# Third of four attentions in passes of 512 tokens, with keys in partitions, maxima by a product and the reciprocal through Ln and Exp

## Chip, core and metric

The kernel runs as one program on one core of a Trainium2 chip. The metric is the device time of one execution in microseconds (us), lower is better. Engines are named as in the profile: PE is TensorE's matmul, PEld its weight load, DVE is VectorE, ACT ScalarE, POOL GpSimd, SP SyncE.

## What is computed

The input x is 4 sequences of 512 tokens with 128 numbers each. Four layers follow, each an attention over a context of 77 tokens per sequence and then a mixture of 8 or 9 experts with the top 2 chosen. The change concerns the attention of layer 2, the third of four:

```python
q1, q2 = heads(x @ q1_w.T), heads(x @ q2_w.T)          # 16 heads of 8
attn1 = softmax(q1 @ k1.T * 8 ** -0.5)                 # over 77 keys
attn2 = softmax(q2 @ k2.T * 8 ** -0.5)
x = (attn1 - (lambda_1 - lambda_2 + 0.1) * attn2) @ v1
x = x * rsqrt(mean(x * x) + 1e-6) * norm_w             # over 128
return x @ proj_w.T + proj_b
```

Here the x that enters is a layer norm, and the result is added to the residual X. The mixture behind it sends each of the 2048 tokens to two experts.

## The kernel before

The 2048 tokens are 16 tiles of 128 (NT), or 4 batches of 512 (NG). Every stage is a set of functions, one for each engine, and the stages are written one after another, so each engine runs its queue in the order in which the code was written, with semaphores between the engines.

`attention_stage("L2x")` runs 32 units, one for each tile and each of the two softmaxes (`sets` is 2). In a unit, `scores` makes 128 tokens by 16 times 77 scores in four PSUM banks, in 12 products: the array is used as four row tiles of 32 (4 heads each), and each product is split into halves (`x_up`, `x_low`) for accuracy. DVE takes the maximum (`maxima`, L971) and subtracts it from PSUM into SBUF (L975), ACT takes the exponential (L1082). PE transposes the result in 11 blocks (L863), ACT copies these out of PSUM (L1105), and PE multiplies them with the values (`weighted`, L874; the array is four column tiles of 32). ACT copies the sums (L1109), PE turns them back to tokens in partitions (L884, L885), DVE divides (L996 to L1014). After the second unit of a tile the difference is squared and summed (L1019), POOL takes the power (`rms`, L1204), ACT scales, PE turns and projects (L899, L900), and DVE adds to X (L1029).

The scores of a unit wait for the DVE's last read of the unit before (`scores_used`). `lead` is the end of the projection of the queries (L693, L711, L719), written between the first units.

`sparse_route("L2f")` is written into the same loop: for groups of tiles that are done it takes statistics, normalises, makes the router's logits, chooses two experts (`choose`, `choose_second`), ranks the tokens (`ranks`, `place`, L1750) and lets POOL scatter the rows to DRAM, sorted by expert (`pool_scatter`, L1799). `parts` are the pieces of the ranking: 8, 4, 2 and 2 tiles, each with two scatters a tile. What belongs to the last tiles stands behind the loop (`late_vector`, `late_pool`), and ends with the table of tiles `tile_at` (L1873). The next stage, the mixture of layer 2, begins on the queue of SP: it reads `tile_at`, loads two packs of weights (L1984), waits for all 32 scatters and loads the sorted rows (L1990).

## Time and profile before

| | |
|---|---|
| median of 3 runs | 1149.68 us (1148.88 to 1149.77) |
| span of the profiled execution | 1167.4 us, the only time that there is of this execution |
| busy: PE, PEld | 956.1 us (82%), 805.2 us (69%) |
| busy: DVE, ACT, POOL | 619.4 us (53%), 559.0 us (48%), 399.0 us (34%) |
| granted TensorE clock, mean | 0.912 of full speed |
| head of the third attention | 500.26 to 512.6 us |
| its loop, up to the last addition to X | 512.6 to 697.55 us |
| from there to the first load of sorted rows | 697.55 to 721.1 us |

The profiled execution is 17.7 us longer than the median. Its clock is a share of the full 2.4 GHz, and in any short stretch it is either that or half of it. A busy PE includes the latency of each product, so it isn't the array at its peak. A group that is not last at the wait that matters costs nothing.

### The profile page before, as it was taken

To read this page: it belongs to the slowest core of one execution; us is meant where nothing else is said; L and a number is where in the kernel's file an instruction comes from. 1 tells how busy PE (TensorE), PEld (TensorE's weight loads), DVE (VectorE), ACT (ScalarE), POOL (GpSimd) and SP (SyncE) were. 2 spreads that over 40 slices of the span, in tenths; PEclk is the share of its full clock that TensorE was granted. 3 is DMA by queue.
4 is the path that set the end of the run, shared out by engine and by line. 5 is a ranking of instruction groups with operands and counts; after the bars stand their busy time and mean duration, and the time that the engine had idled before them with its cause. 6 is when DMAs were issued, how large, how long until landed. Compare 5 with 4: busy or idle time off the path is not lost. (4 is left out here: it accounts for less than half of the span.)

```text
span 1167.4 us, 20624 instructions
## 1 busy us (share of the span) xinstructions
PE 956.1 (82%) x7766; PEld 805.2 (69%) x7766; DVE 619.4 (53%) x1699; ACT 559.0 (48%) x1069; POOL 399.0 (34%) x394
## 2 busy tenths in 40 slices
PE   4888999999988999979888783999367875299992
PEld 3566899999976999846666562989145554288882
DVE  7876412111266343578787653444498763444443
ACT  2666644343446334357665531656245542155552
POOL 4545110000043001500110434547365555545552
PEclk9999999999998999989998875989689985599996
DMA  9999900000000000000000004655200001445543
GB/s 349 183 179 185 199 26 2 1 1 1 1 2 1 1 1 1 1 1 2 1 2 1 28 18 136 201 175 165 73 1 1 1 10 32 137 154 168 170 153 109
DMA packets 70578, 83.83 MB, mean 72 GB/s; under 512 B 5298, under 2 KB 57529, under 8 KB 70353
## 3 DMA queue, kind: packets, MB, share of 16 engines
q1 hardware_dynamic: 64336, 71.98, 26.4%
q0 software_dynamic: 4992, 8.45, 2.1%
q10 hardware_dynamic: 1152, 2.10, 0.5%
q8 instruction: 63, 1.03, 0.4%
q14 instruction: 35, 0.28, 0.1%
HBM read 52.15 MB, written 32.18 MB: 72 GB/s over the span
## 5 line engine op out<-in xcount | busy, mean ns | idle before, releaser
L2374 ACT ACTIVATE hT<-PS,par 128x512 f32<-128x512 f32 x200 | 136.4, 688 | 174.3 <-PE PS L2278 172.8
L2414 DVE SCALAR_TENSOR_TENSOR X<-PS,wts,X 128x128 f32<-128x128 f32 x272 | 76.5, 345 | 218.3 <-PE PS L2297 218.3
L1105 ACT ACTIVATE hT<-PS 116x512 f32<-116x512 f32 (+1 forms) x192 | 102.5, 561 | 108.0 <-PE PS L863 99.4
L863 PE MATMUL PS<-par,score 128*116 128x128 f32 x704 | 114.8, 303 | 23.3 <-DVE oc L1007 12.5
L2297 PEld LDWEIGHTS PS<-regA,hT 128*128 128x128 f32 x1024 | 119.1, 192 | 3.1 <-issue 0.5
L2297 PE MATMUL PS<-regA,hT 128*128 128x128 f32 x1024 | 119.5, 275 | 0.0
L863 PEld LDWEIGHTS PS<-par,score 128*116 128x116 f32 x704 | 85.2, 149 | 41.0 <-issue 31.9
L1179 POOL TENSOR_TENSOR score<-score,mx 128x1232 f32<-128x1232 f32 x32 | 72.0, 2251 | 90.3 <-DVE mx L987 90.3
L2045 PE MATMUL PS<-q_up,halves 128*112 128x256 f32 (+1 forms) x276 | 85.6, 310 | 8.8 <-DVE hT L2154 8.8
L2276 PE MATMUL PS<-x_up,w_halves 128*128 128x512 f32 x200 | 86.4, 432 | 0.2 <-ACT hT L2374 0.2
L1082 ACT ACTIVATE score<-score 128x1232 f32<-128x1232 f32 x64 | 78.3, 1223 | 10.1 <-POOL score L1179 10.1
L2277 PE MATMUL PS<-x_low,w_halves 128*128 128x512 f32 x200 | 80.0, 400 | 0.0
L2278 PE MATMUL PS<-x_up,w_halves 128*128 128x512 f32 x200 | 79.8, 399 | 0.0
L2046 PE MATMUL PS<-q_up,halves 128*112 128x256 f32 (+1 forms) x276 | 79.5, 288 | 0.0
L2047 PE MATMUL PS<-q_up,halves 128*112 128x256 f32 (+1 forms) x276 | 79.4, 288 | 0.0
L874 PE MATMUL PS<-hT,vblk 116*32 116x128 f32 x1408 | 76.8, 293 | 0.1
L2297 PEld LDWEIGHTS PS<-regB,hT 128*128 128x128 f32 x576 | 69.7, 191 | 3.1
L2297 PE MATMUL PS<-regB,hT 128*128 128x128 f32 x576 | 70.1, 275 | 0.0
L594 POOL TENSOR_TENSOR rstd<-vare,mhalf 128x4 f32<-128x4 f32 (+1 forms) x24 | 27.6, 1151 | 114.7 <-DVEq L539 114.7
L874 PEld LDWEIGHTS PS<-hT,vblk 116*32 116x32 f32 x1408 | 53.4, 115 | 18.6 <-issue 8.6
L2213 POOL DMA_INDIRECT sorted_y<-regA x46 | 47.4, 1030 | 53.1 <-DVE regA L2180 42.7
L2213 POOL DMA_INDIRECT sorted_y<-regB x46 | 45.2, 983 | 54.4 <-ACT regB L2119 46.1
(315 smaller groups left out, 2016.2 us busy)
## 6 DMA issues: line engine op xcount, KB each, us to landing
regA<-L3f_w SPq DMA_DIRECT2D x23, 704.0 KB
regB<-L2f_w SPq DMA_DIRECT2D x23, 578.0 KB
L2f_sorted_x<-empty_row SPq DMA_DIRECT2D x8, 1161.0 KB, 21.0
L3f_sorted_x<-empty_row SPq DMA_DIRECT2D x8, 1161.0 KB, 20.2
regA<-L0f_w SPq DMA_DIRECT2D x4, 768.0 KB, 16.9
regA<-L2f_sorted_x SPq DMA_DIRECT2D x23, 129.0 KB, 3.8
regB<-L3f_sorted_x SPq DMA_DIRECT2D x23, 129.0 KB, 4.1
par<-params SPq DMA_DIRECT2D x1, 2450.0 KB, 13.8
```

The lines of the kernel that those rows point to most:

```text
L863: last = nc.tensor.transpose(PS[0:BW, bank_of(("exps", 3 * u + i)), (j % 4) * P:(j % 4) * P + P], exps_of(u)[:, first:first + BW], ident)
L874: last = nc.tensor.matmul(PS[slot, 6, c:c + P], vblk[0:BW, b, j, :], hT[0:BW, u % 2, j // 4, (j % 4) * P:(j % 4) * P + P], start=half == 0 ...
L1105: nc.scalar.activation(hT[0:BW, u % 2, i, 0:width], PS[0:BW, bank, 0:width], ACT.Copy).then_inc(pT_ready.sem, 1)
L2045: nc.tensor.matmul(dst, w_up, up, start=True, stop=False)
L2046: nc.tensor.matmul(dst, w_up, low, start=False, stop=False)
L2047: last = nc.tensor.matmul(dst, w_low_half, up, start=False, stop=True)
L2213: nc.gpsimd.indirect_dma_start(sorted_y, bass.IndirectOffsetOnAxis(ap=at, axis=0), y_slots[:, i % 4, j, :], None, bounds_check=2 * B * S - ...
L2276: nc.tensor.matmul(dst, w_up, upper[:, cols], start=True, stop=False)
L2277: nc.tensor.matmul(dst, w_up, x_low[:, cols], start=False, stop=False)
L2278: last = nc.tensor.matmul(dst, w_low, upper[:, cols], start=False, stop=True)
L2297: last = nc.tensor.matmul(PS[:, 4 + n % 2, j * P:j * P + P], hT[0:rows, n % 2, k, j * P:j * P + P], w2[0:rows, e, k, :], start=k == 0, sto ...
L2374: nc.scalar.activation(hT[:, n % 2, k, :], PS[:, i % 4, :], c["act"], bias=pc(f"{tag}_b1")[:, col:col + 1]).then_inc(h_ready.sem, 1)
```

## The change

The loop of 32 units becomes 8 passes (4 batches by 2 softmaxes), each in 3 steps n, with 3 steps more at the end. In pass i, step k:

- `products` makes scores with up to 103 of the 308 rows (4 heads by 77 keys) in partitions and 512 tokens in columns: 12 products in four row tiles, one PSUM bank each, and 4 more that subtract the maximum, which is a row of `shiftT` times a table of -1 (`minus_head`).
- `exps` takes the exponential from PSUM in two instructions of 1024 columns. There are no transposes of the exponentials.
- `values` and `sums` multiply them, a step later, with the values and with a table of ones for each head, in four column tiles of 512 columns.
- The maximum itself needs scores with tokens in partitions. `maxima` makes them again, 6 products for 8 heads of one tile, 8 times a pass, into banks 4 and 5, which DVE reduces; the maxima of a pass are turned by 4 transposes (`turn`) and copied by ACT (`shift`). They are made one pass ahead.
- `reciprocal` is Ln and Exp(-x) on ACT; DVE's `divide` multiplies numerator and denominator by it, and `correct` does one correction step.
- the square sum is a product with ones, `norm_w` is folded into the projection once, and the bias is added to X by POOL ahead of the passes. Once per batch, `finish` multiplies and adds to X.
- The router's groups are four of 4 tiles, `parts` are 8, 4 and 4, and POOL scatters the 16 rows of part 0 in one piece.
- The tables `minus_head` and `head_cols` add 404 columns to the second load of parameters, and the lambdas take 30 less.

The values of layer 2 are laid out as `vwide`, in the memory of `vblk`. Nothing is changed in the other three attentions, except that layer 3 clears the padding of `vblk` again.

```diff
...
+WIDE = [103, 103, HR * K - 206]
+WIDE_AT = [0, 103, 206]
...
+        def wide_stage(tag, q_ready, kv, nm, lead, sums_read, route):
...
+            passes = B * sets
+            steps = 3 * passes
...
+            def extras(n):
+                i, k = divmod(n, 3)
+                b = finished(i)
+                parts = [[], [], []]
+                if k == 0:
+                    parts[0] += pairs(i + 1, (2,))
+                    parts[1] += pairs(i + 1, (3,))
+                if k == 1:
+                    parts[0] += pairs(i + 1, (4, 5))
+                    parts[1] += pairs(i + 1, (6,))
+                    parts[2] += pairs(i + 1, (7,))
+                    if b is not None:
+                        parts[2].append(("ss", b))
+                if k == 2:
+                    if i + 1 < passes:
+                        parts[0].append(("turn", i + 1))
+                    if b is not None:
+                        parts[0].append(("y", b))
+                    parts[1] += pairs(i + 2, (0,))
+                    parts[2] += pairs(i + 2, (1,))
+                for kind in ("rows", "logits", "ranks"):
+                    if route["due"](kind, n) is not None:
+                        parts[2].append((kind, route["due"](kind, n)))
+                return parts
...
+            head = [("max", p) for p in range(8)] + [("turn", 0)] + [("max", 8), ("max", 9)]
...
+            banks = {"max": (4, 5), "turn": (4,), "ss": (5,), "y": (5,), "rows": (4,), "logits": (5,), "ranks": (4,)}
...
+            def tensor(pe):
+                def maxima(u):
+                    i, p = divmod(u, 8)
+                    (b, s), (j, h) = divmod(i, sets), divmod(p, 2)
+                    t = TG * b + j
...
+                    up, low = q[s]
+                    for m, (half, u_k) in enumerate(((up, 0), (up, 1), (low, 0))):
+                        for r in (2 * h, 2 * h + 1):
+                            dims = slice(32 * r, 32 * r + 32)
+                            last = nc.tensor.matmul(PS[:, 4 + r % 2, 0:HR * K], half[dims, t * P:t * P + P], kb[dims, s, u_k, b, :, :],
+                                                    start=m == 0, stop=m == 2)
+                    last.then_inc(max_psum.sem, 1)
+                def turn(i):
+                    pe.wait_ge(rows_ready.sem, rows_ready.at(TG * (i + 1)))
+                    for j in range(TG):
+                        last = nc.tensor.transpose(PS[:, 4, j * P:j * P + P], max_rows[:, j, :, :].rearrange("p g c -> p (g c)"), ident)
+                    last.then_inc(turn_psum.sem, 1)
+                def products(n):
+                    i, k = divmod(n, 3)
+                    b, s = divmod(i, sets)
+                    up, low = q[s]
+                    w, at, cols = WIDE[k], WIDE_AT[k], slice(512 * b, 512 * b + 512)
+                    if n:
+                        pe.wait_ge(exp_ready.sem, exp_ready.at(n))
+                    for m, (half, u_k) in enumerate(((up, 0), (up, 1), (low, 0))):
+                        for r in range(RG):
+                            dims = slice(32 * r, 32 * r + 32)
+                            nc.tensor.matmul(PS[0:w, r, :], kb[dims, s, u_k, b, :, :].rearrange("p h k -> p (h k)")[:, at:at + w], half[dims, cols],
+                                             start=m == 0, stop=False)
+                    if k == 0:
+                        pe.wait_ge(shift_ready.sem, shift_ready.at(i + 1))
+                    for r in range(RG):
+                        dims = slice(32 * r, 32 * r + 32)
+                        last = nc.tensor.matmul(PS[0:w, r, :], minus_head[dims, at:at + w], shiftT[dims, :], start=False, stop=True)
+                    last.then_inc(prod_ready.sem, 1)
+                def values(n):
+                    i, k = divmod(n, 3)
+                    if k == 0 and i:
+                        pe.wait_ge(sums_used.sem, sums_used.at(i))
+                    pe.wait_ge(exp_ready.sem, exp_ready.at(n + 1))
+                    w = WIDE[k]
+                    for r in range(RG):
+                        nc.tensor.matmul(PS[32 * r:32 * r + 32, 6, :], vwide[0:w, k, i // sets, r, :], hT[0:w, n % 2, r, :],
+                                         start=k == 0, stop=k == 2)
+                def sums(n):
+                    k = n % 3
+                    w = WIDE[k]
+                    for r in range(RG):
+                        last = nc.tensor.matmul(PS[32 * r:32 * r + 32, 7, :], pc("head_cols", w)[:, 32 * k:32 * k + 32], hT[0:w, n % 2, r, :],
+                                                start=k == 0, stop=k == 2)
+                    last.then_inc(sums_psum.sem, 1)
...
+                for use in head:
+                    if use == ("turn", 0):
+                        pe.wait_ge(q_ready.sem, q_ready.at(sets * NG))
...
+                    do(use)
+                    if use == ("max", 1):
+                        lead["transpose_group"](pe, 3)
+                        lead["project"](pe, 2)
+                    if use == ("max", 3):
+                        lead["project"](pe, 3)
+                for n in range(steps + 3):
+                    first, middle, end = extras(n)
+                    if n < steps:
+                        products(n)
+                    for use in first:
+                        do(use)
+                    if 0 < n <= steps:
+                        values(n - 1)
+                    for use in middle:
+                        do(use)
+                    if 0 < n <= steps:
+                        sums(n - 1)
+                    for use in end:
+                        do(use)
...
+            def vector(v, st):
+                def maxima(u):
+                    i, p = divmod(u, 8)
+                    if i >= passes:
+                        return
+                    j, h = divmod(p, 2)
+                    m = mx[:, (u // 2) % 3, :]
+                    v.wait_ge(max_psum.sem, max_psum.at(u + 1))
+                    ps = PS[:, 4:6, 0:HR * K].rearrange("p r (h k) -> p r h k", h=HR)
+                    nc.vector.tensor_reduce(m[:, 8 * h:8 * h + 8].rearrange("p (r h) -> p r h", r=2), ps, AX.X, ALU.max).then_inc(max_read.sem, 1)
+                    if h == 0:
+                        return
+                    v.wait_ge(max_read.sem, max_read.at(u + 1))
+                    if i:
+                        v.wait_ge(turn_psum.sem, turn_psum.at(i))
...
+                    up = max_rows[:, j, :, 0:HR]
+                    nc.vector.tensor_copy(up.bitcast(F32R), m).then_inc(v_step, st.one())
+                    v.wait_ge(v_step, st.n)
+                    nc.vector.tensor_tensor(max_rows[:, j, :, HR:2 * HR], m, up, ALU.subtract).then_inc(rows_ready.sem, 1)
+                def divide(i):
+                    s = i % sets
+                    v.wait_ge(rec_ready.sem, rec_ready.at(i + 1))
...
+                    nc.vector.tensor_tensor(w_check, PS[:, 7, :], w_rec, ALU.mult).then_inc(v_step, st.one())
+                    if s == 0:
+                        ins = nc.vector.tensor_tensor(quotient, PS[:, 6, :], w_rec, ALU.mult)
+                    else:
+                        ins = nc.vector.scalar_tensor_tensor(quotient, PS[:, 6, :], lam[:, 0:1], w_rec, ALU.mult, ALU.mult)
+                    ins.then_inc(sums_used.sem, 1)
+                    v.wait_ge(v_step, st.n)
+                def correct(i):
+                    b, s = divmod(i, sets)
...
+                    nc.vector.scalar_tensor_tensor(quotient, w_check, 2.0, quotient, ALU.subtract, ALU.mult).then_inc(v_step, st.one())
+                    if s == 0:
+                        return
+                    v.wait_ge(v_step, st.n)
...
+                    nc.vector.tensor_tensor(w_att, w_second, w_first, ALU.subtract).then_inc(att_ready.sem, 1)
+                    v.wait_ge(att_ready.sem, att_ready.at(b + 1))
+                    nc.vector.tensor_tensor(w_sq, w_att, w_att, ALU.mult).then_inc(sq_ready.sem, 1)
...
+                def finish(b):
...
+                    v.wait_ge(y_psum.sem, y_psum.at(b + 1))
+                    for j in range(TG):
+                        t = TG * b + j
+                        nc.vector.scalar_tensor_tensor(X[:, t, :], PS[:, 5, j * P:j * P + P], osr[:, j:j + 1], X[:, t, :], ALU.mult, ALU.add)\
+                            .then_inc(x_done.sem, 1)
...
+            def scalar(a, st):
+                def exps(n, h):
...
+                    a.wait_ge(prod_ready.sem, prod_ready.at(n + 1))
+                    if n >= 2:
+                        a.wait_ge(sums_psum.sem, sums_psum.at(n - 1))
+                    ins = nc.scalar.activation(hT[0:w, n % 2, 2 * h:2 * h + 2, :], PS[0:w, 2 * h:2 * h + 2, :], ACT.Exp, scale=scale)
+                    ins.then_inc(*((exp_ready.sem, 1) if h else (a_step, st.one())))
+                def shift(i):
+                    a.wait_ge(turn_psum.sem, turn_psum.at(i + 1))
+                    nc.scalar.activation(shiftT[:, :], PS[:, 4, :], ACT.Copy).then_inc(shift_ready.sem, 1)
+                def reciprocal(i):
+                    a.wait_ge(sums_psum.sem, sums_psum.at(3 * (i + 1)))
+                    if i:
+                        a.wait_ge(sums_used.sem, sums_used.at(i))
+                    nc.scalar.activation(w_ln, PS[:, 7, :], ACT.Ln).then_inc(a_step, st.one())
+                    a.wait_ge(a_step, st.n)
+                    nc.scalar.activation(w_rec, w_ln, ACT.Exp, scale=-1.0).then_inc(rec_ready.sem, 1)
+                nc.scalar.preload_act_table_set("natural_log_exp_and_others")
...
+                shift(0)
+                for n in range(steps + 3):
+                    if n < steps:
+                        exps(n, 0)
+                        if n % 3 == 2 and n // 3 + 1 < passes:
+                            shift(n // 3 + 1)
+                        exps(n, 1)
+                    if n % 3 == 0 and 0 < n <= steps:
+                        reciprocal(n // 3 - 1)
...
+            def pool(p, st):
+                def power(b):
+                    p.wait_ge(ss_read.sem, ss_read.at(b + 1))
...
+                    nc.gpsimd.tensor_tensor(osr[:, :], oss[:, :], mhalf[:, 0:TG], ALU.pow).then_inc(rms_ready.sem, 1)
...
+                for b in range(B):
+                    power(b)
+                    if b < B - 1:
+                        route["pool_power"](p, b)
+                    if b == B - 2:
+                        route["pool_scatter"](p, 0, range(4 * TG))
...
-            groups = {"L2f": [(0, 4), (4, 8), (8, 12), (12, 14), (14, 16)], "L3f": [(0, 4), (4, 8), (8, 12), (12, 16)]}[tag]
-            parts = {"L2f": [(0, 8), (8, 12), (12, 14), (14, 16)], "L3f": [(0, 8), (8, 12), (12, 16)]}[tag]
+            groups = [(0, 4), (4, 8), (8, 12), (12, 16)]
+            parts = [(0, 8), (8, 12), (12, 16)]
             late = len(groups) - 1
             last_part = len(parts) - 1
             step_of = {
-                "L2f": dict(statistics=(10, 18, 26, 30, 34), apply=(11, 19, 27, 31), logits=(12, 20, 28, 32), read=(13, 21, 29, 33),
-                            choose=(21, 29, 33), second=(22, 30, 33), ranks=(23, 31, 34), place=(24, 32)),
+                "L2f": dict(statistics=(8, 14, 20, 26), apply=(9, 15, 21), rows=(10, 16, 22), logits=(11, 17, 23), read=(12, 18, 24),
+                            choose=(18, 24), second=(19, 25), ranks=(20, 26), place=(21,)),
...
-                if tag == "L2f":
-                    pool_scatter(p, 1, range(3))
                 pool_power(p, late)
-                if tag == "L3f":
-                    pool_scatter(p, 1, range(2 * TG))
-                else:
-                    pool_scatter(p, 1, range(3, 8))
-                    pool_scatter(p, 2, range(4))
+                pool_scatter(p, 1, range(2 * TG))
...
```

On PE before, the pattern that every unit of the loop repeats (x_up, x_low and q_up, q_low are the queries of the first and second softmax; L852 is `scores`, L863 the transposes, L874 `weighted`, L884 and L885 the sums turned back):

```order
907 L852 MATMUL PS<-kb,q_low 128x308 x4
908 L863 MATMUL PS<-par,score 116x128 x8
909 L884 MATMUL PS<-par,sums 128x128
910 L885 MATMUL PS<-par,sums 128x64
911 L863 MATMUL PS<-par,score 116x128 x3
912 L874 MATMUL PS<-hT,vblk 32x128 x11
913 L852 MATMUL PS<-kb,x_up 128x308 x8
```

On PE after the change, the second step of pass 1 (L928 and L934 are `products`, L908 is `maxima`, L944 `values`, L951 `sums`):

```order
943 L928 MATMUL PS<-q_up,kb 103x512 x8
944 L928 MATMUL PS<-q_low,kb 103x512 x4
945 L934 MATMUL PS<-shiftT,minus_head 103x512 x4
946 L908 MATMUL PS<-kb,x_up 128x308 x4
947 L908 MATMUL PS<-kb,x_low 128x308 x2
948 L908 MATMUL PS<-kb,x_up 128x308 x4
949 L908 MATMUL PS<-kb,x_low 128x308 x2
950 L944 MATMUL PS<-hT,vwide 32x512 x4
951 L908 MATMUL PS<-kb,x_up 128x308 x4
952 L908 MATMUL PS<-kb,x_low 128x308 x2
953 L951 MATMUL PS<-hT,par 32x512 x4
```

The transposes and the products with 128 columns are gone; products for the maxima of the next pass stand between those of this one. On POOL before, from the first scatter on (L1201 and L1204 are the power of one tile, L1787 that of the router, L1799 the scatters):

```order
108 L1799 DMA L2f_sorted_x<-regA,row_at 20224x129 x4
109 L1201 TENSOR_SCALAR oss<-oss 128x1
110 L1204 TENSOR_TENSOR osr<-oss,mhalf 128x1
111 L1799 DMA L2f_sorted_x<-regA,row_at 20224x129 x4
```

On POOL after (L1161 is `power` of a batch, L2135 the router's, L2147 the scatters):

```order
92 L1161 TENSOR_TENSOR osr<-oss,mhalf 128x4
93 L2135 TENSOR_TENSOR rstd<-vare,mhalf 128x4
94 L2147 DMA L2f_sorted_x<-regA,row_at 20224x129 x16
95 L1161 TENSOR_TENSOR osr<-oss,mhalf 128x4
96 L2135 TENSOR_TENSOR rstd<-vare,mhalf 128x4
97 L2147 DMA L2f_sorted_x<-regA,row_at 20224x129 x16
```

Where four scatters stood between two tiles, 16 now stand ahead of the power of the last batch, and 16 behind it.

## Rows read from the trace of the kernel before

**Rows 1.** Windows: us; busy (x count) PE, PEld, DVE, ACT, POOL; granted clock; DMA.
```profile
500.26:512.60 12.34, 6.38 (x38) 3.01 (x39) 10.21 (x14) 5.58 (x8) 0.00 (x0) 0.95 0.00 1
512.60:562.00 49.40, 45.41 (x513) 32.09 (x513) 39.89 (x60) 34.52 (x62) 2.96 (x8) 0.94 0.01 2
562.00:630.00 68.00, 56.73 (x653) 40.69 (x652) 55.33 (x126) 43.32 (x78) 6.43 (x14) 0.97 0.01 1
630.00:697.55 67.55, 53.83 (x464) 39.77 (x464) 42.89 (x128) 32.40 (x60) 24.21 (x32) 0.81 0.06 18
```

**Rows 2.** Groups by shape, 495 to 700 us: busy us, mean ns.
```profile
L971 DVE TENSOR_REDUCE mx<-PS 128x16 f32<-128x1232 f32 x32 | 46.1, 1440 | 20.0 <-PE PS L852 15.1 <-remote 4.9
L1082 ACT ACTIVATE score<-score 128x1232 f32<-128x1232 f32 x32 | 39.1, 1223 | 0.0
L1105 ACT ACTIVATE hT<-PS 116x512 f32<-116x512 f32 x64 | 35.3, 595 | 48.6 <-PE PS L863 42.6 <-issue 3.5 <-remote 2.6
L719 DVE TENSOR_TENSOR x_low<-PS,x_up 128x512 fp32r<-128x512 f32 x4 | 2.7, 685 | 1.9 <-ACT x_up L711 1.9
```

**Rows 3.** Timeline of one undisturbed unit: start us, us, engine line.
```profile
521.70 1.22 ACT L1082 ACTIVATE score<-score 128x1232 f32<-128x1232 f32 x1
522.41 0.56 PE L852 MATMUL PS<-kb,x_up 32*128 32x308 f32 x8
522.80 0.31 PE L852 MATMUL PS<-kb,x_low 32*128 32x308 f32 x4
523.04 1.09 PE L863 MATMUL PS<-par,score 128*116 128x128 f32 x8
523.16 1.44 DVE L971 TENSOR_REDUCE mx<-PS 128x16 f32<-128x1232 f32 x1 [0.76 <-PE PS L852]
525.89 1.23 ACT L1082 ACTIVATE score<-score 128x1232 f32<-128x1232 f32 x1
```

**Rows 4.** Timeline of the head and of the FFN: products at both clocks and sizes.
```profile
502.70 1.96 PE L693 MATMUL PS<-xnT,par 128*128 128x512 f32 x4 [0.78 <-ACT xnT L650]
511.02 1.44 DVE L975 TENSOR_TENSOR score<-PS,mx 128x1232 f32<-128x1232 f32 x1
512.61 0.89 PE L852 MATMUL PS<-kb,x_up 32*128 32x308 f32 x8 [2.43 <-DVE score L975]
513.80 1.44 DVE L971 TENSOR_REDUCE mx<-PS 128x16 f32<-128x1232 f32 x1 [1.34 <-PE PS L852]
529.60 0.65 PE L874 MATMUL PS<-hT,vblk 116*32 116x128 f32 x16
...
455.98 0.40 PE L2277 MATMUL PS<-x_low,w_halves 128*128 128x512 f32 x1
456.21 0.40 PE L2278 MATMUL PS<-x_up,w_halves 128*128 128x512 f32 x1
```

**Rows 5.** Timeline of DVE: small dependent steps, and four additions to X.
```profile
495.21 1.12 DVE L2414 SCALAR_TENSOR_TENSOR X<-PS,wts,X 128x128 f32<-128x128 f32 x4
702.52 0.17 DVE L1683 TENSOR_REDUCE top<-logits_of 128x2 f32<-128x16 f32 x1
702.73 0.17 DVE L1685 TENSOR_TENSOR picks<-logits_of,top 128x16 f32<-128x16 f32 x1
```

**Rows 6.** Timeline behind the loop: last addition to X, `tile_at`, scatters, SP.
```profile
697.25 0.29 DVE L1029 TENSOR_TENSOR X<-PS,X 128x128 f32<-128x128 f32 x1 [0.29 <-issue]
712.25 0.19 DVE L1873 CAST tile_at<-tile_sums 128x46 int32<-128x46 f32 x1
714.92 0.96 POOL L1799 DMA_INDIRECT L2f_sorted_x<-regA,row_at  x1 [0.30 <-issue]
717.97 0.88 SPq L1984 DMA_DIRECT2D regB<-L2f_w  x2
721.09 0.95 SPq L1990 DMA_DIRECT2D regA<-L2f_sorted_x  x2
```

**Rows 7.** Timeline of POOL ahead of the stage, with the idle time before.
```profile
487.28 1.04 POOL L594 TENSOR_TENSOR rstd<-vare,mhalf 128x4 f32<-128x4 f32 x1 [8.90 <-DVEq L539]
```

410 lines of the change are left out of this document (262 added, 148 removed).

## The prediction

> **What bounds the third attention now.** I read the windows first, since the change touches one stage. Its loop takes 185 us, 512.6 to 697.55, and no engine fills it: in the first 49.4 us PE is marked busy 45.4, DVE 39.9, ACT 34.5; in the last 67.6 us they are 53.8, 42.9 and 32.4 [rows 1]. So waits between engines set the time, and I went to the timeline. In an undisturbed unit one exponential starts 4.19 us after the other; 32 units would take 134 us, and the other 51 us are router work and stretches of low clock [rows 3, 1]. Behind the loop there are two chains. DVE ends `tile_at` at 712.44, SP issues the first weights at 717.97 and the first rows at 721.09; POOL issues its last scatter at 714.92, after 16 in a row, one every 1.26 us (0.96 busy and 0.30 idle), which is 20.2 us for 16 [rows 6].
>
> **Durations.** What the trace shows directly or nearly:
>
> - M, six products for maxima: three times 308 columns as in a unit's scores, of which DVE reads the result 0.75 us after their start; the next product on PE can start after 0.63, of which I put 0.1 down to the change of tile shape [rows 3]. I take 0.53, and 0.1 for each change.
> - R, the reduction of 616 columns: between 1232 columns in 1.44 and 16 in 0.17, so 0.80 [rows 2, 5]. A small dependent step is 0.21, the two that split the maxima 0.42 (c) [rows 5].
> - From the end of a DVE read to the next product, 0.15 [rows 4]. A chain M, R, M, R with nothing else between costs 0.80 + 0.15 + 0.75 = 1.70 a round.
> - V and S, `values` and `sums`: 16 passes of 128 columns in four column tiles take 0.65, so they do run four at once; one full pass of 512 columns takes 1.96 / 4 = 0.49, with latency, so about 0.43. A float32 product is two passes: 0.88 each [rows 4].
> - P, `products`: four rounds of 512 columns, 0.23 a round by the FFN's products, 0.94 in all, readable after 1.15 [rows 4].
> - E, two exponentials of 1024 columns: between 512 in 0.595 and 1232 in 1.223, 1.04 each, 2.0 together; Ln and Exp of 512 columns 1.2; `shift` 0.6 [rows 2].
> - D, `divide`, two times 512 columns on DVE, 1.3; C, `correct`, 0.65, or 1.95 after the second softmax with difference and square [rows 2]. `finish` is 1.12 for four tiles [rows 5].
>
> The array has not run P, V and S in this form. Bounds: P 0.86 by columns at 2.4 GHz alone, 3.7 if the row tiles did not run side by side; V and S 0.85 to 3.4. I take the low ends, since scores with 308 columns and `weighted` run side by side in this trace [rows 3, 4].
>
> On changes of shape, the Trainium skill (TensorEngine Tiling (Array Packing), Key Properties) says that changing the tiling mode drains the engine. The trace shows a gap at such a change, 0.1 us by my reading, not a long one; by the page alone the sum would have no figure for it.
>
> **One pass.** Time 0 is the start of P in the first step. The maxima of the next pass use one pair of banks, so each M waits for the R before it.
>
> - Step 1: last R of the step before ends at 1.0; M at 1.2, R 1.9 to 2.7, M at 2.8, R to 4.4, c to 4.8; V and S lie between, S ends at 4.3; Ln and Exp end at 5.7.
> - Step 2: P 4.3 to 5.2, M, R 5.9 to 6.7, D to 8.0, R to 8.8, c 9.2, C 9.85, R 10.65, M at 10.8, R 11.5 to 12.3, c 12.75. E ends by 7.6 and is not what is waited for.
> - Step 3: P at 11.3; `turn` waits for c, ends at 13.6; `shift` to 14.2; M at 14.4, R 15.1 to 15.9, M at 16.1; the next P at 16.6.
>
> So 16.6 us after a first softmax. After a second one C is 1.3 longer, the square sums are about 0.9, and the projection (0.9) and `finish` (1.12) stand ahead of the M in step 3: 19.6 us. PE changes shape some four times a pass on this path, +0.4. Pass 0 has no D: 15.1. The router's transposes and logits take banks 4 and 5 in passes 3 and 5, +3.7, and the statistics ahead of them hold back an R, +1.1. Passes 0 to 6: 15.1 + 16.6 + 19.6 + 21.4 + 19.6 + 21.4 + 19.5 = 133.2, with 0.4 x 7 = 2.8, **136**. The loop of before at 4.19 would be 134 for all 32 units, so per token little is gained; what is saved is router work, which in 512-token steps stands in the way less often.
>
> **Head.** Before, 12.3 us [rows 1]. Now all eight M of pass 0, the turn and two M of pass 1 precede the first P. Ten rounds of 1.70 are 17.0; three of them are 0.9 longer, since the split and two copies of the projection (0.42 + 2 x 0.68 [rows 2]) outlast the 0.9 that they hide; turn and shift add 1.4: P starts 21.1 us after 500.26. With PE waiting for so much of it, I expect the low clock, as at 512: there the result comes after 513.80 - 512.61 = 1.19 instead of 0.75 [rows 4]; for six rounds +2.6, and the first P +1. **24.7**.
>
> **Tail.** Pass 7 has no maxima. Its steps take about 3.2 us each, so the mean squares of the last batch would be ready some 17.5 us after its start. But POOL has 16 scatters ahead of their power. The places of part 0 are ready at 2.6; 2.6 + 16 x 1.26 = 22.8, power 1.04 [rows 7], `finish` 1.12: the last X at **25.3**, about 5 us of them for that queue.
>
> **Behind the loop.** 721.09 - 697.54 = 23.55 before [rows 6]. With four tiles instead of two in the last group: statistics, power and normalising +1.5, transposes and copy +0.65, logits at the low clock +1.0, choosing and ranks +1.3: +4.4. The scatters' chain, 5.9 to the first places, 16 x 1.26 = 20.2, landing about 2, comes out the same. **28**.
>
> **Nothing.** POOL's three new operations stand where it was idle for 8.9 us, about 3 of them used; without this cover they would cost 3 [rows 7]. The bias lies in POOL's idle time in the head (0.00 busy [rows 1]). The 374 more columns of parameters are not waited for in a row that I found.
>
> **Sum.** 24.7 + 136 + 25.3 + 28 = 214.0. The loop has had its clock at 0.94, 0.97 and 0.81 [rows 1]; for stretches at half speed I add 3: 217. Before 721.09 - 500.26 = 220.8. So 3.8 us less, of 1167.4 in the profiled execution, whose time outside its span isn't known and which is 17.7 us above the median. I take the difference off the median: **1146 us**. A measurement of this kernel can tell about 0.2%, 2.3 us.
>
> **Rivals.**
>
> 1. More is hidden than I think, faster (0.18). Between the first P and pass 7 DVE has 54 R (43), 27 c (11), D and C (19), finishes and router work (16): 89 us, where my chain has 136. If PE kept half of that ahead, 23 us would go: 1123. For it: V and S lie between the M. Against it: one pair of banks, so only what DVE does between two R can hide an M.
> 2. The clock, slower (0.17). At half speed a pass costs six times 0.44 for M, two P and three V or S on the path twice as long, about 7 us more. PE is used 12.9 of 16.6 us by my ledger (three P, V and S, eight M, the turn), in short pieces. If 4 of 10 stretches were at half speed, it would be 8 x 7 x 0.4 = 22, with 3 in the sum already: 1165. It decides once about 7 us are added, an eighth of the passes' time beyond mine. For it: in the last third of the loop, where PE waits for router work, the clock was 0.81 [rows 1]. Against it: 0.94 to 0.97 in the rest with similar gaps. The Trainium skill (TensorE: Matmul & The Clock Gate, A second HAM failure mode: psum-queue depth-cycling) tells of a kernel where short idle times between groups of products, from cycling through PSUM banks, made the clock swing. That is this rival; by that page it would be likelier than 0.17.
> 3. The tiles don't run side by side at 512 columns (0.08), slower. P alone at its bound adds 2.8 x 24 = 66; if it is V and S by a half more, 0.44 x 4 on the path x 8 = 14: 1160 or far beyond.
> 4. POOL's and DVE's queues behind the loop are longer (0.05): power or places late by 10: 1156.
>
> My case has 0.52, with its own range 1137 to 1154: faster 0.33, same 0.10, slower 0.09. In all: faster 0.51, same 0.11, slower 0.38. The range for 8 in 10 reaches into the first three rivals: 1127 to 1168.
>
> **What would show it.** R near 0.80, 64 of them; M to R 0.75; a pass of 17 to 21 us; PE idle mostly for R and `shift`; the last 16 scatters ending some 26 us behind the last X; POOL busy with scatters when the last mean squares are done. Wrong: P far over 1 us, a clock under 0.85 from 525 to 660, ACT waited for in step 2, or passes under 14 us.

## The result, and the profile after

The changed kernel takes 1187.6 us (median of 4 runs, 1185.55 to 1190.61) against 1149.72 (4 runs, 1148.88 to 1149.92): 1.0337 times the time before, 95% interval 1.0318 to 1.0356. It is slower by 37.9 us, where I had 3.7 us less and a range up to 1168. Its profiled execution has a time of 1187.65 us and a span of 1185.8.

The windows of the stage, cut at the first M, at the first P of each of the eight passes, at the last addition to X and at the first load of sorted rows (columns as in [rows 1]):

```profile
501.05:529.60 28.55, 17.82 (x75) 9.85 (x74) 14.79 (x28) 5.58 (x9) 3.28 (x4) 0.60 0.00 1
529.60:550.50 20.90, 19.02 (x136) 10.95 (x136) 7.89 (x17) 6.37 (x7) 0.00 (x0) 0.57 0.00 1
550.50:566.90 16.40, 14.52 (x151) 6.94 (x152) 9.49 (x19) 7.53 (x9) 0.00 (x0) 1.00 0.00 1
566.90:589.20 22.30, 18.31 (x172) 9.99 (x168) 12.13 (x26) 7.53 (x9) 1.02 (x1) 0.92 0.00 1
589.20:614.60 25.40, 21.12 (x166) 10.29 (x166) 12.99 (x35) 8.54 (x11) 1.01 (x1) 0.80 0.01 2
614.60:641.80 27.20, 24.84 (x164) 12.57 (x163) 11.18 (x24) 7.64 (x9) 1.01 (x1) 0.62 0.00 1
641.80:668.80 27.00, 22.71 (x170) 10.96 (x170) 13.01 (x35) 8.76 (x11) 1.01 (x1) 0.75 0.01 1
668.80:695.10 26.30, 23.87 (x165) 13.17 (x164) 14.93 (x49) 7.64 (x9) 1.51 (x2) 0.68 0.00 1
695.10:721.45 26.35, 19.29 (x147) 10.12 (x146) 12.07 (x40) 9.33 (x12) 17.21 (x18) 0.81 0.13 41
721.45:749.20 27.75, 7.75 (x34) 6.96 (x33) 13.38 (x67) 2.59 (x5) 16.43 (x17) 0.50 0.24 81
```

Against the ledger: head 28.55 (24.7), seven passes 165.5 (136, and 3 for the clock), tail 26.35 (25.3), behind the loop 27.75 (28); 248.1 in all where I had 217. One pass, the second, ran wholly at the full level of the clock (2.4 GHz) and took 16.4 us, 17.0 by the ledger. The others had a granted clock of 0.57 to 0.92, that is, up to 86% of their time at the lower level of 1.2 GHz, and took up to 27.2. The loop of before had 0.94, 0.97 and 0.81 [rows 1]. From 525 to 660 us the clock was 0.75, which was one of my signs of being wrong ("under 0.85").

The groups by shape, 501 to 721.5 us, show that the durations were as forecast: R 798 ns and 64 of them, E 1.02 us, Ln and Exp 0.60 and 0.63. They replace the R, Exp and copies of [rows 2]. DVE idled 78.0 us for M's results ahead of R:

```profile
L1024 DVE TENSOR_REDUCE mx<-PS 128x8 f32<-128x616 f32 x64 | 51.0, 798 | 78.4 <-PE PS L908 78.0
L1117 ACT ACTIVATE hT<-PS 103x1024 f32<-103x1024 f32 x32 | 31.0, 1019 | 37.4 <-PE PS L934 37.3
L1043 DVE TENSOR_TENSOR w_check<-PS,score 128x512 f32<-128x512 f32 x8 | 5.5, 682 | 3.7 <-ACT score L1131 3.7
L1131 ACT ACTIVATE score<-score 128x512 f32<-128x512 f32 x8 | 5.0, 630 | 0.3
L1129 ACT ACTIVATE score<-PS 128x512 f32<-128x512 f32 x8 | 4.8, 598 | 18.0 <-PE PS L951 18.0
```

The same step of a pass at both levels of the clock (timeline, start us, us). First in the third pass, at the full one. P takes 1.0 us up to the next product, then comes an M, and DVE waits 1.30 for it before R. The next M starts after PE has been idle for 0.95, and DVE goes on with D:

```profile
571.74 0.72 PE L928 MATMUL PS<-x_up,kb 32*103 32x512 f32 x8
572.29 0.41 PE L928 MATMUL PS<-x_low,kb 32*103 32x512 f32 x4
572.52 0.42 PE L934 MATMUL PS<-shiftT,minus_head 32*103 32x512 f32 x4
573.38 0.80 DVE L1024 TENSOR_REDUCE mx<-PS 128x8 f32<-128x616 f32 x1 [1.30 <-PE PS L908]
574.28 0.55 PE L908 MATMUL PS<-kb,q_up 32*128 32x308 f32 x4 [0.95 <-DVE mx L1024]
574.69 0.74 DVE L1047 SCALAR_TENSOR_TENSOR score<-PS,lam,score 128x512 f32<-128x512 f32 x1
```

And in the fifth, at the lower one up to 622.8 us: V and S are 1.94 us each (1.06 at the full level), all products follow each other without a gap, and R waits 2.94:

```profile
616.29 1.94 PE L944 MATMUL PS<-hT,vwide 102*32 102x512 f32 x8
618.15 0.88 PE L908 MATMUL PS<-kb,q_up 32*128 32x308 f32 x4
619.22 1.94 PE L951 MATMUL PS<-hT,par 102*32 102x512 f32 x8
621.09 1.19 PE L928 MATMUL PS<-x_up,kb 32*103 32x512 f32 x8
622.86 0.45 PE L908 MATMUL PS<-kb,q_up 32*128 32x308 f32 x4
623.49 0.80 DVE L1024 TENSOR_REDUCE mx<-PS 128x8 f32<-128x616 f32 x1 [2.94 <-PE PS L908]
```

What matters is who waits: at the full clock PE waits for R (0.95), at the lower one DVE waits for PE. The busy share of a whole pass hides this (14.52 of 16.40 us, and 24.84 of 27.20). It shows when the stretches are cut where the clock changes, here one at the full level and one at the lower:

```profile
547.60:581.90 34.30, 28.81 (x286) 13.83 (x284) 20.34 (x40) 14.36 (x18) 0.00 (x0) 1.00 0.00 1
626.20:639.90 13.70, 12.80 (x72) 7.26 (x64) 5.54 (x15) 2.54 (x3) 1.01 (x1) 0.50 0.00 1
```

PE is busy 84% of the first and 93% of the second (81% and 93% over all such stretches of the seven passes). TensorE has become the bound there by being half as fast, not by having more to do.

### The profile page after: what moved, and what is told of

It reads as the page before. It is cut to its first block and busy times, and to the rows that moved or that the text cites. A ratio compares the mean times of both kernels' runs of the same rounds, so it can differ in the third digit from the quotient of the medians.

```text
span 1185.8 us, 19765 instructions
## 1 busy us (share of the span) xinstructions
PE 972.9 (82%) x7400; PEld 781.0 (66%) x7400; DVE 581.3 (49%) x1650; ACT 512.0 (43%) x947; POOL 396.0 (33%) x372
## 3 DMA queue, kind: packets, MB, share of 16 engines
q1 hardware_dynamic: 64336, 72.17, 25.1%
## 5 line engine op out<-in xcount | busy, mean ns | idle before, releaser
L1024 DVE TENSOR_REDUCE mx<-PS 128x8 f32<-128x616 f32 x64 | 51.0, 798 | 78.4 <-PE PS L908 78.0
L1117 ACT ACTIVATE hT<-PS 103x1024 f32<-103x1024 f32 (+1 forms) x48 | 47.2, 1020 | 83.0 <-PE PS L934 82.9
L1488 ACT ACTIVATE hT<-PS 116x512 f32<-116x512 f32 (+1 forms) x96 | 51.3, 562 | 47.2 <-PE PS L1283 45.8
L1283 PE MATMUL PS<-par,score 128*116 128x128 f32 x352 | 56.0, 296 | 14.4 <-DVE oc L1411 11.7
L2382 PEld LDWEIGHTS PS<-q_up,halves 128*112 128x112 f32 (+1 forms) x276 | 52.0, 188 | 14.0 <-DVE hT L2491 13.1
L1161 POOL TENSOR_TENSOR osr<-oss,mhalf 128x4 f32<-128x4 f32 x4 | 4.1, 1018 | 159.7 <-DVE oss L1071 159.7
## 6 DMA issues: line engine op xcount, KB each, us to landing
par<-params SPq DMA_DIRECT2D x1, 2637.0 KB, 13.7
```

The source lines that it names most:

```text
L1283: last = nc.tensor.transpose(PS[0:BW, bank_of(("exps", 3 * u + i)), (j % 4) * P:(j % 4) * P + P], exps_of(u)[:, first:first + BW], ident)
L2382: nc.tensor.matmul(dst, w_up, up, start=True, stop=False)
```

## The experiments

The chips differ: on some the kernel before takes 1149 to 1151 us, on others 1165 to 1170, so each time is given as a ratio to the kernel before on the same chip. The two theories: **clock** (the passes are as forecast at full clock; the low clock lengthened them) and **chain** (M and R over one pair of banks take some 25 us a pass at any clock).

### Bases: how large is the loss in this stage?

The kernel before and the changed one, unedited.

> The kernel before, unchanged, profiled once more. The first profile of it was 17.7 us above its own median, and it is what the sum of the prediction was set against. Under the theory that the third attention is where the difference lies, the time from the end of the second attention to the first rows (220.8 us in the first profile) is about the same here, 215 to 222, and the missing 18 us come from other stages. If it is 203 or less, the whole comparison of this stage was against a slow profile, and the change lost more in this stage than the two profiles say.

> The kernel before, profiled on the chip of the changed kernel's profile of this call. If this chip runs it in about 1150 us, its third attention with what follows up to the first rows takes 205 to 212 us where the two earlier profiles have 220.8 and 217.2, and the change loses 36 to 43 us there. If it takes 217 or more again, the change loses about 31 us there and the other 7 elsewhere.

> The kernel before, profiled once more. If this chip runs it in about 1150 us, the stage up to the first rows is 207 to 213 us long, since the changed kernel has 248 there on such chips and the whole differs by 38. If it is a chip of 1165 to 1170 us, 217 to 221 as in the three profiles so far.

> The changed kernel unchanged, as the base for the others of this call: the earlier call ran on a chip where the kernel before took 1170 us, 1.8% more than where the change was timed, and had no run of the changed kernel beside it. Expected is the known ratio, 1.034 times the kernel before on the same chip. If the ratio is well above that on a chip where the kernel before is slow too, the changed kernel suffers more from whatever makes that chip slow; the clock theory expects that, with a lower granted clock in the loop, the theory of a chain that costs the same at any clock does not.

> The changed kernel unchanged, as the base of this call: 1.031 to 1.034 times the kernel before, as in the two comparisons so far. On a chip where the kernel before is slow (1170 us) the clock theory expects a higher ratio, since there the clock is lower.

> The changed kernel as base of this call, 1.031 to 1.035 times the kernel before, with 248 to 251 us from the first M to the first rows.

The changed kernel took 1187.4, 1188.9 and 1208.3 us: 1.031 (1.026 to 1.036), 1.035 (1.031 to 1.039) and 1.037 (1.032 to 1.042) times the kernel before. The higher ratio that the clock theory expected on a chip of 1170 us isn't clear of the noise, and what a2_after has more lies mostly in its tail (below); its passes take 167.0 us where the changed kernel has 165.5. From its first M to the first rows it has 262.2 us, not the 248 to 251 that I expected.

The window from the first M (here of any form) to the first rows in the kernel before, e0_before_3 first, then e0_before_again:

```profile
500.86:708.47 207.61, 161.99 (x1696) 115.75 (x1696) 158.54 (x382) 116.43 (x211) 47.77 (x69) 0.90 0.05 17
```
```profile
501.70:719.62 217.92, 169.16 (x1696) 121.54 (x1696) 158.63 (x382) 116.60 (x211) 47.90 (x69) 0.87 0.05 15
```

e0_before has 217.2, also on a chip of 1170 us. That and the 217.9 here came out inside my expectations, and for a while made the wrong reading likely, that the missing 18 us lie elsewhere; e0_before_3 settled it. On a chip of 1150 us this stage is 207.6 us long, not the 220.8 that I compared with: 13.2 of the 21.7 us by which the first profile's span was longer lay right in this stage. With 248.1 after, the loss there is 40.5, and the spans (1185.8 and 1145.7) differ by 40.1: all of it is here. Each chip was used once, so chip and occasion can't be told apart. One thing that the executions of 1165 us and more have, and those of 1150 don't, are waits that the trace puts down to "remote", in which several engines stand still together. In the first profile they cost R 4.9 us [rows 2], and none in e0_before_3. In a2_after one lies in the tail, 19.03 us on DVE and 4.45 on ACT, and tail and rest are 65.9 us instead of 54.1:

```profile
722.21 0.19 DVE L2006 TENSOR_TENSOR logits_of<-PS,par 128x32 f32<-128x32 f32 x1 [19.03 <-remote]
```

What the engines wait for there wasn't tried.

### Idle products in every wait

```
 if kind in ("max", "turn") and bank is not None:
+    for _ in range(2):           # and 4
+        nc.tensor.matmul(PS[:, bank, 0:512], zeros, x_up[:, 0:256].bitcast(BF16), start=False, stop=False)
```

> The changed kernel with two idle products more (zero weights of 128x128 in bfloat16, 512 columns, added into the banks of values or sums, so the result stays) ahead of the wait of six of the eight maxima products of a pass and of the turn. They need about 0.23 us each at full clock and lie where TensorE waits 0.5 to 1 us for DVE. Clock theory (the passes are as forecast at full clock, and the loss is that TensorE falls to the low clock): granted clock in the loop rises from 0.74 to over 0.9, a pass takes 17 to 22 us instead of 25 to 27, and the whole is 15 to 35 us less, 1153 to 1173. Rival (the chain of products and reductions over one pair of banks costs 25 us a pass at any clock): the clock may rise, but passes stay at 24 us or more, and the time is 1180 to 1200.

> As the kernel with two idle products, with four at each place: 0.9 us of filling, about as long as the longest waits. Clock theory: the clock is at least as high as with two, but some filling is on the path (about 0.3 us at 7 places in 7 passes, 15 us), so the time lies between that of two and that of the changed kernel: 1165 to 1185. Rival (the chain): 1190 to 1215. If neither dose moves the granted clock, the filling is no test of the clock and something other than gaps sets it.

Measured on a chip of 1170 us: 1238.4 us, 1.057 (1.052 to 1.062), with two, and 1230.6, 1.051 (1.046 to 1.056), with four. Both are slower than the changed kernel (1.037 on another such chip; the kernel with four was not timed beside it on one chip). So much of the filling was on the path: V or S lies in most of the waits already. With two, the clock of the seven passes was 0.70, not over 0.9 but below the changed kernel's 0.75: this forecast failed. With four it was 0.85. Four cost no more than two (the 8 us between them are within the scatter of four runs each), though they are some 22 us more of products, and the fifth pass (window) tells why, with two and with four:

```profile
637.10:669.50 32.40, 29.28 (x170) 13.83 (x172) 11.22 (x24) 7.63 (x9) 1.01 (x1) 0.63 0.00 1
```
```profile
643.30:668.40 25.10, 22.27 (x184) 10.52 (x186) 11.18 (x24) 7.53 (x9) 1.01 (x1) 1.00 0.00 1
```

With more products in it, the pass is 7.3 us shorter at the full level of the clock. It has 28 idle products; four of them take 0.97 us up to the next product (647.01 to 647.98), 6.8 in all. So without them it would last between 18.3 and 25.1 us, where the changed kernel had 27.2 at 0.62 and the forecast was 20.0. This alone doesn't rule out a chain of 25 us; the same pass with nothing added, 22.8 us at 0.78 in e4_bias_late (below), does. The absolute times that I expected (1153 to 1185) didn't come; as ratios they stand for 1215 and 1208 on a chip of 1150 us, the second in the rival's range.

### No first making of the scores

```
-    return [("max", 8 * i + p) for p in ps] if i < passes else []
+    return []
```

> The changed kernel without its first making of the scores: no product for maxima, no reduction, no split, so a shift of zero (the scores are scaled down by ten so that the exponentials stay finite; the output is not the reference's). What is left of a step is P, E and the next P, about 0.94 + 0.2 + 2.04 + 0.15 = 3.3 us, 10 a pass with some router work on top, 85 for the loop; the head is 5 us. By my durations at full clock the maxima cost 136 - 85 in the loop and some 19 in the head, 70 in all. If the time falls by 65 to 80 against the changed kernel, the maxima cost what the ledger said and the low clock is a loss of the whole stage that stays here too; if by 100 to 120, then the maxima are also what brought the low clock, by the waits that they make. The granted clock of the loop tells which: 0.9 or more here, or still about 0.75.

1097.5 us, 0.953 (0.949 to 0.957): 89.9 less than the changed kernel beside it, between my two figures. The fourth to sixth pass:

```profile
547.60:560.30 12.70, 11.17 (x116) 4.89 (x112) 3.90 (x14) 8.59 (x11) 1.01 (x1) 1.00 0.00 1
560.30:573.90 13.60, 11.59 (x121) 5.43 (x121) 5.45 (x15) 7.47 (x9) 1.01 (x1) 1.00 0.00 1
573.90:586.60 12.70, 11.18 (x120) 4.86 (x116) 3.87 (x14) 8.58 (x11) 1.01 (x1) 1.00 0.00 0
```

The first six passes are all at 1.00, the seventh, with the router's work, at 0.74; the seven take 93.5 us where the forecast had 85. So most of the low clock came with the maxima. Whether by their M or by the waits for R the run doesn't tell, since it takes out both, and the seventh pass shows that it can fall without them.

### The reciprocal on DVE again

```
+ nc.vector.reciprocal(w_rec, PS[:, 7, :])
- nc.vector.tensor_tensor(w_check, PS[:, 7, :], w_rec, ALU.mult)     # and Ln, Exp, the correction
```

> The changed kernel with one part undone: the reciprocal of the sums is made by DVE in one operation on 128x512, and Ln, Exp, the product for the check and the correction are left out (DVE loses two operations of 0.68 us a pass, ACT two of 0.6). No row shows what this reciprocal costs; from 0.65 us (as a copy) to some 4 us (several steps an element). At 0.65 each pass is about 0.7 us shorter on DVE: 5 us less in all, 1182. At 4 us: each pass 2.6 us longer, 21 us more, 1208. Under the clock theory a longer idle time of TensorE in step 2 also keeps the clock low.

1239.7 us, 1.060 (1.053 to 1.068), against 1.037 for the changed kernel on another such chip: about 27 us more, above my upper figure of 21, with 107 us at the lower clock in the seven passes instead of 92 (2 x (1 - clock) x length, added up over the windows of the passes; against a2_after). The operation takes 3.35 us:

```profile
557.58 3.35 DVE L1043 RECIPROCAL score<-PS 128x512 f32<-128x512 f32 x1
```

Taking Ln, Exp and the correction for it saves 8 x (3.35 - 1.37) = 16 us of DVE. This part of the change is a gain.

### The bias later

```
+ if g == 0:
+     p.wait_ge(rows_ready.sem, rows_ready.at(TG))
```

> The changed kernel with POOL's addition of the bias held back until the first four rows of maxima are split (about 18 us later), so that it no longer runs beside DVE's normalising at the start of the stage. There DVE took 2.53 us for four pieces that take 1.11 elsewhere. If POOL's running beside it is the cause, these four pieces take 1.1 here and the first reduction starts 1.4 us sooner, and TG reductions beside the moved addition show whether DVE's reads of PSUM are slowed too (above 0.80). If it is not, they stay at 2.5. The whole moves by -1.5 us at most, less than a run tells.

1185.5 us (2 runs), 1.030 (1.025 to 1.035), the same as the changed kernel. In the changed kernel, DVE's four pieces beside POOL's addition, and the first R; below, in this one:

```profile
500.04 3.20 POOL L1166 TENSOR_TENSOR X<-X,par 128x512 f32<-128x512 f32 x3
501.31 2.53 DVE L572 TENSOR_SCALAR xn<-X,mv,rstd 128x128 f32<-128x128 f32 x4
503.76 0.79 DVE L1024 TENSOR_REDUCE mx<-PS 128x8 f32<-128x616 f32 x1
```
```profile
504.14 1.11 DVE L572 TENSOR_SCALAR xn<-X,mv,rstd 128x128 f32<-128x128 f32 x4
505.17 0.79 DVE L1024 TENSOR_REDUCE mx<-PS 128x8 f32<-128x616 f32 x1
...
522.22 4.23 POOL L1168 TENSOR_TENSOR X<-X,par 128x512 f32<-128x512 f32 x4 [19.31 <-DVE score L1036]
525.24 0.80 DVE L1024 TENSOR_REDUCE mx<-PS 128x8 f32<-128x616 f32 x1 [3.10 <-PE PS L908]
```

2.53 became 1.11, and the R that lies wholly beside POOL's addition now takes 0.80 like the others: this read of PSUM wasn't slowed. The head was 22.3 us at a clock of 0.85 instead of 28.5 at 0.60, but its first pass then 23.1 at 0.50: the clock fell later, and the sum stayed (192.6 us for head and passes, 194.1 before).

### Shorter M, and a second pair of banks in the head

```
- for m, (half, u_k) in enumerate(((up, 0), (up, 1), (low, 0))):    # e5: one round
+ last = nc.tensor.matmul(PS[:, 4 + r % 2, 0:HR * K], up[dims, t * P:t * P + P], kb[dims, s, 0, b, :, :], start=True, stop=True)
+ def first_bank(u): return 2 if u in (3, 5, 7) else 4              # e6: banks 2 and 3
```

> The changed kernel with the maxima taken from one round of products (upper halves only) instead of three, and without the lower half of their split: the shift is then a little off, the same for all keys of a head, so it cancels in the quotient. M is ready 0.23 to 0.35 us sooner, c is 0.21 instead of 0.42. On the chain that sets the time stand 10 M in the head and about 7 in each of 7 passes: 59 x 0.35 = 21 us at full clock, half as much again at the clock of 0.74, and 4 for c: 20 to 35 us less than the changed kernel. If instead DVE's other work sets the passes, 5 or less. If less work on TensorE in the same waits pulls the clock down further (under 0.7), the gain is eaten: 0 to 15.

> The changed kernel with a second pair of banks for three of the eight M of the head (those of index 3, 5 and 7 use banks 2 and 3, free until the first P). An M then needs not wait for the R just before it in five rounds, which saves up to 0.9 us a round at full clock (0.15 + 0.75) and 1.4 at the low one; copies for the projection lie between some: 4 to 7 us less than the changed kernel. If the head is bound by DVE and the projection instead, 0 to 2.

> One round of products for the maxima, the second pair of banks in the head, and the late bias, together. If their gains add: 19 + 5 + 1 = 25 us less than the changed kernel, about 1162; if less idle time in the head also keeps the clock up in the first passes, up to 35 less, 1152. The kernel before, at 1150, would not be beaten.

> One round of products for the maxima, the second pair of banks in the head and the late bias, together, once more as base: 1.004 to 1.009 times the kernel before on a chip of 1150 us, 1.010 to 1.018 on one of 1170.

One round: 1168.5 us, 1.017 (1.012 to 1.022), 18.8 less than the changed kernel beside it and just under the forecast of 20 to 35; its second pass, at 1.00, is 14.3 us instead of 16.4. Banks: 1184.2, 1.034 (1.028 to 1.041); the runs don't tell 4.8 us, but the traces of two otherwise equal kernels on one chip do, 29.53 us of head against 22.92, with the other windows alike within 0.1:

```profile
501.47:531.00 29.53, 18.82 (x73) 10.14 (x72) 14.78 (x28) 5.58 (x9) 3.27 (x4) 0.57 0.00 1
```
```profile
501.48:524.40 22.92, 13.50 (x71) 7.21 (x71) 14.41 (x28) 5.58 (x9) 3.28 (x4) 0.74 0.00 1
```

All three edits: 1156.4, 1.0066 (1.0042 to 1.0091), and again 1155.8, 1.0049 (1.0030 to 1.0069). That is 32.5 less than the changed kernel, more than the 25 of the three gains added up, with 64 us at the lower clock in the seven passes instead of 83.

### Idle products in the long waits alone

```
+ {"max": 4, "ss": 3}.get(use[0], 0) if ends else 0     # ahead of the last M and the square sums; 2 ahead of the turn, 3 in the head
```

> The changed kernel with idle products (zero weights, 512 columns of bfloat16, 0.23 us each at full clock) only where TensorE waits about as long: three ahead of each of the last five entries of the head, two ahead of the turn (0.47 us of wait), and in passes with a finished batch four ahead of the last M (1.25) and three ahead of the square sums (0.89). About 11 us of products in all. Clock theory: part of the falls go, above all those at the end of the step with the finished batch, the granted clock of the loop rises from 0.74 by 0.05 to 0.2, and the time falls by 5 to 25 us against the changed kernel, though work was added. Rival (low clock is a companion of the long passes and not their cause): clock up or not, the time rises by 0 to 11. If the clock doesn't move, the run tells nothing of it.

> The kernel with one round for the maxima, second banks in the head and the late bias, plus the same idle products. It stood at 1.0066 times the kernel before, with a loop clock of 0.80. Clock theory: 5 to 15 us less, 0.993 to 1.002 times the kernel before. Rival: the same or up to 11 us more, 1.007 to 1.016.

1.036 (1.031 to 1.041) where the changed kernel beside it has 1.037, and 1.015 (1.008 to 1.021). The seven passes together are 170.0 us against 167.0, with 79 us at the lower level against 92 (2 x (1 - clock) x length, over the rows). So the clock rose a little, as expected, from 0.73 to 0.77, but the time didn't fall by 5 to 25 us: 1211.3 against 1208.3, and 1.015 where I expected 1.010 to 1.018 without filling on such a chip. Both times lie where the rival (0 to 11 more) had them. By the price worked out below, 13 us less of low clock are worth 5, which the filling ate; the times alone don't show it. The first pass, where only two idle products lie, is the clean piece; in a2_after and here:

```profile
529.70:549.90 20.20, 18.14 (x134) 10.48 (x134) 7.91 (x17) 6.30 (x7) 0.00 (x0) 0.60 0.00 1
```
```profile
531.40:547.90 16.50, 14.57 (x137) 7.56 (x138) 7.90 (x17) 6.35 (x7) 0.00 (x0) 0.90 0.00 1
```

Nothing but the clock, and two products more, sets these two apart. As a cure filling is of no use here; why the clock falls in one pass and not in its like is not settled.

### Without the correction

```
- nc.vector.tensor_tensor(w_check, PS[:, 7, :], w_rec, ALU.mult)
- nc.vector.scalar_tensor_tensor(quotient, w_check, 2.0, quotient, ALU.subtract, ALU.mult)
```

> The same kernel without the correction of the reciprocal: DVE loses the check product and the correction (0.69 us each) in every softmax; the quotient is then as exact as Ln and Exp are. By the ledger both lie on the chain of step 2, which DVE fills: 8 x 1.38 = 11 us less than the kernel beside it, and 0.995 to 1.000 times the kernel before. Rival (the passes are bound by TensorE at the low clock, and DVE's two operations lie in its shadow): 0 to 4 us less, and not below the kernel before.

1143.1 us (12 runs), 0.9935 (0.9913 to 0.9957): 0.65% faster than the kernel before, and 12.7 less than the same kernel with the correction, give or take 2, which fits the 11 forecast. But only a part is DVE's own time on the path: the second pass at 1.00 is 13.7 us against 14.3 (e5), 0.6 for 1.38 of DVE's work. The loop's seven passes are 131.8 us instead of 145.8, and their time at the lower level 39 us instead of 64; at 0.4 a us that is 10 of the 14. Its third to sixth pass:

```profile
550.50:571.00 20.50, 17.56 (x140) 9.29 (x136) 10.14 (x20) 7.53 (x9) 1.02 (x1) 0.83 0.00 1
571.00:593.80 22.80, 18.77 (x138) 8.08 (x134) 10.96 (x28) 8.65 (x11) 1.01 (x1) 0.78 0.01 1
593.80:612.50 18.70, 15.67 (x135) 7.69 (x134) 9.40 (x19) 7.53 (x9) 1.01 (x1) 0.91 0.00 1
612.50:631.20 18.70, 14.62 (x132) 6.42 (x130) 10.96 (x28) 8.54 (x11) 1.01 (x1) 1.00 0.00 1
```

## Why the prediction was wrong

**The step that failed: "for stretches at half speed I add 3".** Six profiled executions of passes with the same instructions, at different clocks, give the price. With low time = 2 x (1 - clock) x length: the second pass is 16.4 us at 1.00, 18.9 at 0.82 (6.8 low) and 20.5 at 0.72 (11.5 low), 0.36 us longer for each us of low time. The fifth is 22.8 at 0.78 (10.0 low), 27.2 at 0.62 (20.7) and 28.9 at 0.56 (25.4): 0.40, which puts it at 18.8 without any. The second and the fifth in e4_bias_late, and the fifth in a1_after:

```profile
549.30:569.80 20.50, 19.09 (x155) 9.33 (x152) 9.49 (x19) 7.53 (x9) 0.00 (x0) 0.72 0.00 1
...
620.20:643.00 22.80, 20.07 (x159) 10.82 (x158) 11.18 (x24) 7.53 (x9) 1.01 (x1) 0.78 0.00 1
```
```profile
620.00:648.90 28.90, 26.62 (x163) 13.94 (x162) 11.27 (x24) 7.64 (x9) 1.01 (x1) 0.56 0.00 1
```

In the changed kernel the low time of the seven passes is 83 us, half of them; 83 x 0.4 = 33, and 165.5 - 33 = 132. My 136 was right within 3%: 18.8 where I had 20.0, 16.4 for 17.0. This is an extrapolation. The price of a us of low time lies between 0.27 and 0.46 from pass to pass, and no other pass ran at 1.00; but each of the seven, carried to no low time by its own six executions, comes within 2.2 us of the ledger, and together they make 132 too. The term for the clock had to be about 30 and was 3.

Rival 2 named it and was short in both factors: "4 of 10 stretches" were 5 of 10, and "about 7 us more" a pass is 10 to 13 (0.36 and 0.40 a us of low time mean a pass 1.6 to 1.7 times as long when all of it is low: 16.4 becomes 26, 18.8 becomes 31). I counted only the products on the full-clock path. My own ledger had the bound: TensorE is used 12.9 of 16.6 us, so at half speed it alone needs 25.8. The chance of 0.17 was too low as well. "Against it: 0.94 to 0.97 in the rest with similar gaps" [rows 1] failed: the gaps there were between other products, and no row told how those between M and R would do. The Trainium skill (TensorE: Matmul & The Clock Gate, A second HAM failure mode: psum-queue depth-cycling) says that short idle times between groups of products make the clock oscillate. The trace agrees that it does: the clock changes its level 17 times between 529 and 695 us. What makes it fall at one place and not at another stays open.

**The second: "I take the difference off the median".** The profile of before, in its span 21.7 us longer than e0_before_3, had 13.2 of that in this very stage. Against 207.6 even my 217 was 9 us slower, 1159. The sign of my forecast hung on that. With the 31.1 us by which the stage exceeds my 217, it makes 44.3 between the forecast and the profiles; the medians have 41.6.

**Head, 24.7: 28.5.** 1.4 of it is POOL's bias, which I put under **Nothing** because POOL was idle; that DVE's normalising beside it would take 2.53 instead of 1.11 I hadn't asked. The rest is the clock, 0.60 over the whole head instead of six rounds. At 0.85 and without the bias it was 22.3.

**Tail, 25.3: 26.35, for another reason.** The terms that I listed make 25.0; 0.3 of the 25.3 has no source. The scatters' queue was to cost 5. POOL's last scatter of that part ends at 717.96, DVE hands over the mean squares at 718.05, and the power waits 0.18:

```profile
717.00 0.96 POOL L2147 DMA_INDIRECT L2f_sorted_x<-regA,row_at  x1 [0.30 <-issue]
718.14 1.04 POOL L1161 TENSOR_TENSOR osr<-oss,mhalf 128x4 f32<-128x4 f32 x1 [0.18 <-DVE oss L1071]
720.33 1.12 DVE L1079 SCALAR_TENSOR_TENSOR X<-PS,osr,X 128x128 f32<-128x128 f32 x4 [0.23 <-PE PS L965]
```

The steps of the pass at a clock of 0.81 took as long as the queue, so that both end together. **Behind the loop** 28 was 27.75, against [rows 6].

**Rivals 1, 3 and 4** are out: the one pass at full clock took 16.4 of the ledger's 17.0, so little more was hidden, P took 1.0 us and V and S 1.06 at full clock, so all tiles ran side by side, and nothing was late behind the loop.

## What to carry to other kernels

Price a change twice, at either level of TensorE's clock: what the path takes at full clock, and TensorE's own work doubled. Here the second was far above the first (25.8 against 16.6 us a pass), TensorE stood in a chain with DVE, and the clock was the largest term. There, shortening DVE's link paid: 12.7 us for two operations of 0.69 us in eight softmaxes, most of it by less time at the lower clock. Never take a stage from a profile that is slower than the timed runs without asking whether the excess lies in that stage.

A shift of a softmax need not be exact: one round of products for the maxima instead of three gave 18.8 us.

## What the runs showed of the hardware

A normalising of four 128x128 tiles on DVE takes 2.53 us while POOL adds over 128x512, 1.11 without it; a DVE reduction that reads PSUM stays at 0.80 beside the same addition. A reciprocal of 128x512 from PSUM takes DVE 3.35 us, Ln and Exp 0.60 and 0.63 on ACT. The kernel before takes 1150 us on some chips and 1170 on others, 1.7% more, and the profiles of 1165 us and more have waits put down to "remote", up to 5 us each (19 in the changed kernel); their cause wasn't tried. The same pass with the same instructions took 27.2 us at a granted clock of 0.62 and 22.8 at 0.78.
